# Moving the sums' loads to ScalarE, a wider use of the first slot group, fewer scatters between the last moves, and a bias added by DMA

## The chip, the core and the metric

The program runs on one core of one Trainium2 chip. The metric is the time of one execution in device microseconds (us), as the median of several runs. One execution was also recorded by the profiler; all rows below come from it.

## The reference, cut to what matters

The input `x` holds 8 sequences of 512 tokens with 256 numbers each (4096 tokens). Two layers follow each other, each with a layer norm ahead of it and a residual around it:

```python
x = x + attention(_layernorm(x), ...)        # only the first 16 rows of each sequence attend; every other row gets the bias "ob"
x = x + ffn(_layernorm(x), ...)              # per token: 4 of 32 experts and one shared expert
```

Inside `ffn` a router picks 4 experts for each token (`topk_idx`) and gives each a weight (`topk_w`). An expert is `down @ (silu(gate @ t) * (up @ t))` with an inner width of 128. The four results are multiplied by their weights, added, and the shared expert (width 256) is added on top. So there are 4096 * 4 = 16384 (token, expert) pairs.

For all rows but the first 16 of a sequence the attention gives zero, so that the first residual is `x + ob` with the bias row `ob`.

## The kernel before

The 4096 tokens are 32 tiles of 128. Tile 0 holds the 16 rows of each sequence that attend; tiles 1 to 31 hold the rest. `x_sb` keeps all of x in SBUF. x is loaded in five groups of tiles (`GROUPS_OF_TILES`, line 50): 1-4, 5-8, 9-16, 17-24 and 25-31; groups are counted from 0.

The work has two stages that overlap. In the **first stage** (0 to about 180 us) TensorE, ScalarE and VectorE do the attention of tile 0 as a chain of steps, and fill the time between the steps with other work in an order written out by hand (`FILL_PE`, `FILL_ACT`, `FILL_DVE`, lines 156 to 235). A letter with a number is an item: on VectorE `N0` to `N5` are the statistics of groups 3 and 4 (`statistic`, line 1543: bias, moments, root), `R` the pieces of the routing, `U` the products of the shared expert, `A` its additions. `N0` and `N3` add `ob` to the 8 and 7 tiles of groups 3 and 4 with one instruction each (`add_bias`, line 1277).

Every token row is then copied four times into DRAM, to a slot in the region of each of its experts. That is a **move**: ScalarE lays the normalised rows and their pair numbers into one of four groups of buffers in `xg` (`stage`, line 829), and GpSimd sends them out with four indirect DMAs per tile (`move(n)`, line 743, n = 0 to 31, tile 0 last). The 16 places of `xg` serve twice: moves use them as four groups of four, and the second stage loads its tiles into them.

In the **second stage**, the loop over expert tiles u (`part`), each u is 128 rows of one expert. 137 of them (`FIXED`) are certain. For each u, SyncE loads the rows from DRAM into a place of `xg` (`load_tile`, line 588), TensorE transposes them (`turn_x`, line 1175), multiplies by gate and up (`gate_up_of`) and by down (`down_of`), ScalarE copies and applies Silu (`keep_x`, `gate`, `keep_y`), VectorE copies the weights and makes the product (`hidden`), and GpSimd sends the result rows to `pairs_dram` with one indirect DMA, a **scatter** (`scatter(u)`, line 762). TensorE's order in the loop is gate and up of u, down of u - 1, turn of u + 2. The first 32 tiles need only the moves of token tiles 1 to 16; all later ones need every move. `place_of` (line 75) says which place a tile is loaded into: the first 24 go to places 0 to 7 (move groups 0 and 1), later ones around all 16. A place that held a tile before is free when that tile has been turned and its pair numbers kept (u below 63) or scattered (u from 63); a place that only moves have used is free when all the moves of its group have landed.

GpSimd's queue is one fixed order (lines 773 to 778): moves 0 to 28, then scatters between the last moves as `SOON` tells, then all other scatters.

The **sums**: VectorE adds the four weighted pair rows of a token tile to `x_sb` (`add_rows`, line 1805), in pairs of token tiles at the loop positions `SUM_AT`. The rows come back by loads of 512 KB into five buffers (`load_rows`, line 609). Ten pairs of such loads stand in SyncE's queue between its tile loads, at the positions `LOAD_AT` (79, 84, 90, ...); the first of them waits until every scatter below u = 63 has landed. SyncE also clears 128 rows behind each expert's region (`make_blank`, two per tile at u = 9 to 24), and stores finished groups.

```python
def place_of(u):
    return u % (RING // 2) if u < FIRST_LAPS else u % RING     # RING = 16, FIRST_LAPS = 24
```

Of the kernel before, what the change touches and what calls it, by code (L numbers as in the profile page):

```python
# [25 lines left out]
ALU = mybir.AluOpType  # L26
# [3 lines left out]
P = 128  # L30
# [4 lines left out]
TT = TOKENS // P  # L35
# [33 lines left out]
NARROW = 24  # L69


FIRST_LAPS = RING + RING // 2


def place_of(u):
# [24 lines left out]
KEPT = 63  # L100
# [18 lines left out]
def outs_used(k, n):  # L119
# [11 lines left out]
BEFORE_END = 24  # L131
SUM_ORDER = [*range(1, BEFORE_END + 1), 0, *range(BEFORE_END + 1, TT)]
EARLY_LOADS = 5
LOAD_AT = [79, 84, 90, 96, 110, 116, 121, 126, 131, 135]
assert STAGES[:2] == [PARTS[0][1] - 1, PARTS[1][1] - 1] and STAGES[3] == BEFORE_END and DONE_BY[3] < FIXED
assert all(at - RING + 1 >= DONE_BY[[2 * pair + 2 <= t for t in STAGES].index(True)] for pair, at in enumerate(LOAD_AT))
assert SUM_AT[-1] + TOPK <= FIXED and LOAD_AT[-1] < FIXED
SOON = {TT - 3: 4, TT - 2: 9, TT - 1: 14}
RANK_STEP = 2
STAGE_IN_LOOP = {0: 25, 2: 26, 5: 27, 8: 28, 11: 29, 15: 30, 18: 31}  # L140
ADD_IN_LOOP = {1: 12, 7: 13, 13: 14, 17: 15}
# [67 lines left out]
]  # L209
FILL_DVE = [  # L210
    "R0 R0 N6 R0 R0 R0 R0 P0 P1 P2 R0 R0 N0 U0 N1 N2 U1",
    "N3 N4 N5 R1 R1 R1",
    "R1 R1 R1 U2 U3",
    "R1",
    "U4 R1",
# [64 lines left out]
def build_program(nc, x, qkvo, gate_up, down, sh_gate_up, sh_down, router, rows, cols, local, out,  # L280
                  tokens_dram, pairs_dram):
    ctx = ExitStack()
    with ctx:
# [3 lines left out]
        def sem(name):  # L287
            return ctx.enter_context(nc.semaphore(name))
# [132 lines left out]

        att_x_in = sem("att_x_in")
        x_in = [sem(f"x_in{g}") for g in range(len(GROUPS_OF_TILES))]
        ob_in = sem("ob_in")
        router_in = sem("router_in")
        small_in = sem("small_in")
# [99 lines left out]
        def _(sp):  # L526
# [81 lines left out]

            def load_rows(q):

                if q == 0:
                    sp.wait_ge(pair_added, SHARED + 1)
                    for k in range(SHARED_OUTS[-1] + 1):
                        sp.wait_ge(scattered[k], 16 * outs_used(k, KEPT))
                elif q == 2:
                    sp.wait_ge(hid_ready, WEIGHTS_FROM + 2 * (3 * TOPK + 2) + 1)
                if q < BEFORE_END:
                    if q >= EARLY_LOADS:
                        sp.wait_ge(tile_summed, q - EARLY_LOADS + 1)
                    sp.dma_start(early4[q % EARLY_LOADS].rearrange("p k d -> p (k d)"), pair_tiles[:, SUM_ORDER[q], :]  # L620
                                 ).then_inc(early_in[q % EARLY_LOADS], 16)
                else:
                    sp.dma_start(load4[:, q - BEFORE_END].rearrange("p k d -> p (k d)"), pair_tiles[:, SUM_ORDER[q], :]
                                 ).then_inc(pairs_in[q - BEFORE_END], 16)
# [6 lines left out]
            for u in range(FIXED):  # L631
                if u == EARLY:
                    sp.wait_ge(moved_last, 16 * TOPK)
                    sp.wait_ge(tables_ready, 2)
                    sp.wait_ge(blanked, 16 * E)
                load_tile(u)
                for e in range(E):
                    if BLANKS_AT[e] == u:
                        make_blank(e)
                if u in LOAD_AT:  # L640
                    load_rows(2 * LOAD_AT.index(u))
                    load_rows(2 * LOAD_AT.index(u) + 1)
                if u == LOAD_AT[4]:
                    sp.wait_ge(tile_summed, 8)
                    store(*OUT_GROUPS[0])

# [30 lines left out]
        def _(pool):  # L677
# [60 lines left out]
            assert made[0] == N_CONSTS  # L738
            for what in ROOTS[3:]:
                inverse_root(what)  # L740


            def move(n):
# [50 lines left out]
        def _(act):  # L794
# [120 lines left out]
            def keep_y(u):  # L915
# [6 lines left out]
                    act.wait_ge(pair_added, 15)  # L922
                act.activation(yb[out_of(u)], y_ps(u), ACT.Copy).then_inc(y_ready, 1)  # L923

            def part(a, b):

                keep_x(a)
                keep_x(a + 1)
                for u in range(a, b):
                    if u in STAGE_IN_LOOP:  # L930
                        stage(STAGE_IN_LOOP[u])
                    gate(u)
                    if u > a:
                        keep_y(u - 1)
                    if u + 2 < b:
                        keep_x(u + 2)
                    if u == SHARE_STEP:
                        act.wait_ge(gate_done, SHARED + 1)
                        act.activation(pair_hid_0.rearrange("p m t -> p (m t)"), gate_0_ps, ACT.Silu
                                       ).then_inc(pair_silu_done, 1)  # L940
                keep_y(b - 1)
# [309 lines left out]
        def _(dve):  # L1251
# [291 lines left out]
            def statistic(k):  # L1543

                a, b = GROUPS_OF_TILES[3 + k // 3 % 2]
                if k in (0, 3):
                    add_bias(3 + k // 3)
                elif k in (1, 4):
                    moments(3 + k // 3)
                elif k == 6:  # L1550
                    shifts(*GROUPS_OF_TILES[2])
                else:
                    seq(dve.tensor_scalar(var_e[:, a:b], mv[:, a:b, 1:2].rearrange("p t a -> p (t a)"), EPS, None, ALU.add))
                    newton(rstd[:, a:b], var_e[:, a:b], half_root[:, 0:b - a])
                    dve.scalar_tensor_tensor(shift[:, a:b], mv[:, a:b, 0:1].rearrange("p t a -> p (t a)"), -1.0,
                                             rstd[:, a:b], ALU.mult, ALU.mult).then_inc(norm_ready, 1)
# [372 lines left out]
```

## Time and profile before

| | us |
|---|---|
| median of 3 runs | 443.57 |
| lowest and highest run | 441.66, 443.99 |
| the profiled execution | 442.9 |
| its span, first to last instruction | 441.1 |
| TensorE busy in the span | 363.4 (82%) |
| VectorE, ScalarE, GpSimd busy | 303.3, 238.5, 301.9 |

Engine names in the profile: PE is TensorE's matmul, PEld its weight load, DVE VectorE, ACT ScalarE, POOL GpSimd, SP SyncE; a q behind a name means its instruction queue. Times in rows are us from the start of the span unless marked ns. In a timeline a row is: start, length, engine, line, operation, out<-in, form, count, and in brackets the idle time before it with what ended it.

### The profile page before, as it was taken

The numbers are of one execution on the slowest core, as the hardware profiler recorded it, in microseconds if no ns is written. First come the engines' busy times: TensorE is split into PE (matmuls) and PEld (weight loads), VectorE is DVE, ScalarE is ACT, GpSimd is POOL, SyncE is SP. The second block draws the span as 40 slices with busy tenths as digits, with TensorE's granted clock in tenths as the row PEclk, the third lists the DMA queues.
The fourth block names the chain that finished last, engine by engine and source line by source line (L and its number), as shares of the span: only waits on it lengthen the run. The fifth ranks groups of instructions, "written<-read, shape, count | busy, mean of one in ns | idle before, by whom it ended". The sixth has DMA issues, their size and how long they took to land.

```text
span 441.1 us, 9457 instructions
## 1 busy us (share of the span) xinstructions
PE 363.4 (82%) x2368; PEld 295.4 (67%) x2368; DVE 303.3 (69%) x1097; ACT 238.5 (54%) x612; POOL 301.9 (68%) x438
## 2 busy tenths in 40 slices
PE   0468899999788898799959999999999999999200
PEld 0354666757346455588849899999989989998200
DVE  3669995963997965367524468885477847887847
ACT  1454693578564656557725566556555656655100
POOL 5511888677887887877878777777777776666300
PEclk9999996999999999999989999999999999999855
DMA  7990233432228968778965885652798898997796
GB/s 168 250 332 24 90 115 115 155 119 92 111 103 330 397 243 273 266 234 274 291 200 170 274 241 152 186 173 97 255 308 282 293 328 278 340 292 250 264 309 214
DMA packets 47033, 98.01 MB, mean 222 GB/s; under 512 B 8697, under 2 KB 30846, under 8 KB 45696
## 3 DMA queue, kind: packets, MB, share of 16 engines
q1 hardware_dynamic: 33968, 62.70, 45.9%
q0 software_dynamic: 12720, 34.62, 21.1%
q8 instruction: 23, 0.38, 0.4%
q14 instruction: 34, 0.28, 0.2%
q10 hardware_dynamic: 288, 0.03, 0.1%
HBM read 53.93 MB, written 44.57 MB: 223 GB/s over the span
## 4 chain that ended last, share of the span: by engine, by line
PE 63%; DVE 15%; DMA 9%; issue 4%; ACT 3%; POOL 3%; SPq 1%; POOLq 0%; DVEq 0%; ACTq 0%
PE two_banks L1192 24%; PE two_banks L1205 12%; PE two_banks L1016 7%; PE two_banks L1179 6%; PE two_banks L1067 5%; DMA loopb<-slots_dram 3%; PE two_banks L971 3%; DVE x_sb L1816 3%; DMA slots_dram<-loopb,slot_i 2%; PE two_banks L965 2%; DMA gu_w<-pairs_dram 1%; DMA pairs_dram<-routing,loopb 1%; POOL pairs_dram L766 1%; PE two_banks L1151 1%; DVE loopb L1599 1%
## 5 line engine op out<-in xcount | busy, mean ns | idle before, releaser
L756 POOL DMA_INDIRECT slots_dram<-loopb,slot_i x128 | 129.0, 1008 | 49.3 <-issue 25.4
L1192 PE MATMUL two_banks<-routing,staged_w 128*128 128x128 f32 x1096 | 145.8, 276 | 0.1
L1192 PEld LDWEIGHTS two_banks<-routing,staged_w 128*128 128x128 f32 x1096 | 134.1, 193 | 0.4 <-ACT routing L908 0.4
L1205 PE MATMUL two_banks<-dn_w,routing 128*128 x274 | 83.3, 386 | 1.5 <-DVE routing L1802 1.3
L1802 DVE TENSOR_TENSOR routing<-routing,two_banks 128x128 f32<-128x128 f32 x137 | 39.1, 286 | 65.6 <-ACT routing L913 59.2
L1842 DVE COPY staged_w<-gu_w 128x512 f32 x137 | 62.2, 455 | 15.7 <-issue 12.4
L913 ACT ACTIVATE routing<-two_banks 128x128 f32<-128x128 f32 x137 | 38.0, 277 | 57.6 <-PE two_banks L1192 57.5
L1016 PE MATMUL two_banks<-gu_w,sgu_w 128*128 128x512 f32 (+1 forms) x128 | 63.1, 624 | 3.1 <-DVE loopb L1599 2.3
L1179 PE MATMUL two_banks<-ident,loopb 128*128 128x128 f32 x274 | 52.9, 275 | 10.3 <-DMA loopb<-slots_dram 8.9
L908 ACT ACTIVATE routing<-two_banks 128x256 f32<-128x256 f32 x137 | 52.0, 380 | 13.3 <-PE two_banks L1179 13.3
L766 POOL DMA_INDIRECT pairs_dram<-routing,loopb x44 | 45.7, 1038 | 17.4 <-issue 15.3
L1179 PEld LDWEIGHTS two_banks<-ident,loopb 128*128 128x128 f32 x274 | 38.0, 142 | 26.0 <-DMA loopb<-slots_dram 10.7
L1205 PEld LDWEIGHTS two_banks<-dn_w,routing 128*128 128x128 f32 x274 | 41.8, 193 | 3.4 <-issue 3.0
L766 POOL DMA_INDIRECT pairs_dram<-routing,stats x33 | 35.0, 1059 | 9.7 <-issue 7.3
L841 ACT ACTIVATE loopb<-x_sb,shift,rstd 128x1024 f32<-128x1024 f32 x32 | 39.5, 1234 | 2.8 <-DMA slots_dram<-loopb,slot_i 2.7
L1016 PEld LDWEIGHTS two_banks<-gu_w,sgu_w 128*128 128x128 f32 x128 | 24.0, 203 | 25.2 <-issue 18.4
L923 ACT ACTIVATE routing<-two_banks 128x256 f32<-128x256 f32 x77 | 29.6, 384 | 13.9 <-PE two_banks L1205 13.9
L965 PE MATMUL two_banks<-ident,gu_w 128*128 128x128 f32 x62 | 14.8, 337 | 22.2 <-POOL gu_w L736 15.9
L1067 PE MATMUL two_banks<-sdn_w,loopb 128*128 128x256 f32 x124 | 30.2, 386 | 3.2 <-ACT gu_w L880 1.3
L965 PEld LDWEIGHTS two_banks<-ident,gu_w 128*128 128x128 f32 x62 | 9.8, 183 | 28.5 <-POOL gu_w L736 15.8
L1067 PEld LDWEIGHTS two_banks<-sdn_w,loopb 128*128 128x128 f32 x124 | 22.6, 190 | 8.5 <-issue 3.5
L766 POOL DMA_INDIRECT pairs_dram<-sgu_w,loopb x20 | 20.0, 999 | 8.2 <-issue 7.5
(302 smaller groups left out, 514.6 us busy)
## 6 DMA issues: line engine op xcount, KB each, us to landing
loopb<-slots_dram SPq DMA_DIRECT2D x137, 128.5 KB, 2.8
routing<-pairs_dram SPq DMA_DIRECT2D x14, 512.0 KB, 5.3
loopb<-pairs_dram SPq DMA_DIRECT2D x10, 512.0 KB, 4.4
slots_dram<-blank SPq DMA_DIRECT2D x33, 136.0 KB, 27.1
gu_w<-in_gate_up SPq DMA_DIRECT2D x2, 2048.0 KB, 10.7
gu_w<-pairs_dram SPq DMA_DIRECT2D x8, 512.0 KB, 7.8
gu_w<-in_gate_up SPq DMA_DIRECT2D x6, 512.0 KB
x_sb<-in_x SPq DMA_DIRECT2D x2, 1024.0 KB, 13.9
```

The source lines that it names most:

```text
L756: pool.indirect_dma_start(out=slots_dram, out_offset=bass.IndirectOffsetOnAxis(ap=slot_i[:, at:at + 1], axis=0), in_=xg[:, r, :] if n < TT ...
L766: pool.indirect_dma_start(out=pairs_dram, out_offset=bass.IndirectOffsetOnAxis(ap=(kept_ids[:, u:u + 1] if u < KEPT else xg[:, place_of(u) ...
L841: act.activation(rows_of[:, :, 0:D], x_sb[:, t, :].unsqueeze(1).to_broadcast([P, TOPK, D]), ACT.Identity, bias=shift[:, t:t + 1], scale=rs ...
L908: act.activation(xT[:, u % 2], turn_ps[u % 2], ACT.Copy).then_inc(xT_ready, 1)
L913: act.activation(silu[:, u % 2, 0:I], bank[2 + u % 2][:, 0:I], ACT.Silu).then_inc(silu_done, 1)
L1016: ins = pe.matmul(o[:, 0:n], weights[:, m, c, :], xnT[:, 4 * q:4 * q + n // P, c, :], start=(c == 0), stop=(c == KC - 1))
L1067: ins = pe.matmul(pair_y_ps[:, i, :], pair_hid[:, m, t:t + P], sdn_w[:, m, :], start=(m == 0), stop=(m == 1))
L1179: ins = pe.transpose(turn_ps[u % 2][:, c, :], xg[:, place_of(u), c * P:(c + 1) * P], ident[:, :])
L1192: ins = pe.matmul(bank[2 + u % 2][:, m * P:(m + 1) * P], staged_w[:, u % 2, c, m * I:(m + 1) * I], xT[:, u % 2, c, :], start=(c == 0), sto ...
L1205: ins = pe.matmul(y_ps(u), hid[:, u % 2, 0:P], w, start=True, stop=True)
L1802: dve.tensor_tensor(hid[:, u % 2, 0:I], silu[:, u % 2, 0:I], bank[2 + u % 2][:, I:2 * I], ALU.mult).then_inc(hid_ready, 1)
L1842: dve.tensor_copy(staged_w[:, u % 2].rearrange("p c i -> p (c i)"), gu_w[:, bass.ds(ids[first][u % EIDS], 1)].rearrange("p a c i -> p (a c ...
```

## The change

There are four parts. Ten pairs of sums' loads leave SyncE's queue for ScalarE's, where they stand ahead of `gate(u)` at slightly smaller positions, with their waits; the store of tiles 1 to 8 stays in SyncE's queue at u = 116. Tiles 24 to 31 are loaded into places 0 to 7. Eight scatters instead of fourteen stand between the last moves. The two bias additions of groups 3 and 4 leave VectorE; GpSimd issues two DMAs that add the bias row to `x_sb` in flight, after its own constants and roots and ahead of move 0, and VectorE waits for them ahead of the moments.

```diff
-FIRST_LAPS = RING + RING // 2
+FIRST_LAPS = 2 * RING
...
-LOAD_AT = [79, 84, 90, 96, 110, 116, 121, 126, 131, 135]
+LOAD_AT = [76, 81, 86, 91, 104, 109, 114, 119, 124, 129]
+STORE_AT = 116
...
-SOON = {TT - 3: 4, TT - 2: 9, TT - 1: 14}
+SOON = {TT - 3: 2, TT - 2: 5, TT - 1: 8}
...
-    "R0 R0 N6 R0 R0 R0 R0 P0 P1 P2 R0 R0 N0 U0 N1 N2 U1",
-    "N3 N4 N5 R1 R1 R1",
+    "R0 R0 N6 R0 R0 R0 R0 P0 P1 P2 R0 R0 U0 N1 N2 U1",
+    "N4 N5 R1 R1 R1",
...
+        bias_added = [sem(f"bias_added{g}") for g in (3, 4)]
...
             def load_rows(q):
 
-                if q == 0:
-                    sp.wait_ge(pair_added, SHARED + 1)
-                    for k in range(SHARED_OUTS[-1] + 1):
-                        sp.wait_ge(scattered[k], 16 * outs_used(k, KEPT))
-                elif q == 2:
-                    sp.wait_ge(hid_ready, WEIGHTS_FROM + 2 * (3 * TOPK + 2) + 1)
...
-                if u in LOAD_AT:
-                    load_rows(2 * LOAD_AT.index(u))
-                    load_rows(2 * LOAD_AT.index(u) + 1)
-                if u == LOAD_AT[4]:
+                if u == STORE_AT:
                     sp.wait_ge(tile_summed, 8)
                     store(*OUT_GROUPS[0])
...
+            for g, (a, b) in list(enumerate(GROUPS_OF_TILES))[3:]:
+                pool.wait_ge(ob_in, 16)
+                pool.wait_ge(x_in[g], 16)
+                pool.dma_start(x_sb[:, a:b, :], row("ob").unsqueeze(1).to_broadcast([P, b - a, D]), accum_op=ALU.add
+                               ).then_inc(bias_added[g - 3], 16)
...
+            def load_early(q):
+
+                if q == 0:
+                    act.wait_ge(pair_added, SHARED + 1)
+                    for k in range(SHARED_OUTS[-1] + 1):
+                        act.wait_ge(scattered[k], 16 * outs_used(k, KEPT))
+                elif q == 2:
+                    act.wait_ge(hid_ready, WEIGHTS_FROM + 2 * (3 * TOPK + 2) + 1)
+                for stage_of, t in enumerate(STAGES[:2]):
+                    if q == t:
+                        for k in OUTS:
+                            act.wait_ge(scattered[k], 16 * outs_used(k, DONE_BY[stage_of + 1]))
+                if q >= EARLY_LOADS:
+                    act.wait_ge(tile_summed, q - EARLY_LOADS + 1)
+                act.dma_start(early4[q % EARLY_LOADS].rearrange("p k d -> p (k d)"), pair_tiles[:, SUM_ORDER[q], :]
+                              ).then_inc(early_in[q % EARLY_LOADS], 16)
+
             def part(a, b):
...
                 for u in range(a, b):
+                    if u in LOAD_AT:
+                        load_early(2 * LOAD_AT.index(u))
+                        load_early(2 * LOAD_AT.index(u) + 1)
...
                     gate(u)
...
-                if k in (0, 3):
-                    add_bias(3 + k // 3)
-                elif k in (1, 4):
+                if k in (1, 4):
+                    dve.wait_ge(bias_added[k // 3], 16)
                     moments(3 + k // 3)
```

## Rows read from the trace of the kernel before

**Rows 1.** Busy time by stretch: length, busy us (count) by engine, PE clock, DMA share, GB/s.

```profile
260.00:280.00 20.00, 20.00 (x157) 18.69 (x157) 16.87 (x54) 12.10 (x40) 15.73 (x15) 1.00 0.58 172
...
228.60:231.60 3.00, 3.00 (x12) 2.75 (x13) 0.26 (x2) 0.66 (x2) 2.39 (x3) 0.50 0.85 243
```

**Rows 2.** Timeline of PE: around tiles 24, 32, 79 and 85, and at 51 us.

```profile
222.52 0.60 PE L1205 MATMUL two_banks<-dn_w,routing 128*128 x2
228.60 0.69 PE L1179 MATMUL two_banks<-ident,loopb 128*128 128x128 f32 x2 [5.49 <-DMA loopb<-slots_dram]
...
243.76 0.44 PE L1179 MATMUL two_banks<-ident,loopb 128*128 128x128 f32 x2 [1.09 <-DMA loopb<-slots_dram]
...
316.47 0.38 PE L1179 MATMUL two_banks<-ident,loopb 128*128 128x128 f32 x2
...
326.80 0.44 PE L1179 MATMUL two_banks<-ident,loopb 128*128 128x128 f32 x2 [0.86 <-DMA loopb<-slots_dram]
...
51.37 1.99 PE L1067 MATMUL two_banks<-sdn_w,loopb 128*128 128x256 f32 x8 [0.32 <-DVE loopb L1599]
```

**Rows 3.** The chain of waits, its transfers: start, length, what.

```profile
238.69 2.43 DMA slots_dram<-loopb,slot_i
...
241.60 2.12 DMA loopb<-slots_dram
...
321.29 5.47 DMA loopb<-slots_dram
```

**Rows 4.** Timeline of POOL around its last moves: scatters (L766) and moves (L756).

```profile
206.59 1.03 POOL L766 DMA_INDIRECT pairs_dram<-routing,stats  x1 [0.19 <-issue]
...
211.80 0.97 POOL L756 DMA_INDIRECT slots_dram<-loopb,slot_i  x1 [0.30 <-ACT loopb L923]
...
216.87 1.00 POOL L766 DMA_INDIRECT pairs_dram<-routing,stats  x1 [0.19 <-issue]
```

**Rows 5.** Timeline of SP's queue: blanks, tile loads (L599) and sums' loads (L620).

```profile
219.77 0.85 SPq L576 DMA_DIRECT2D slots_dram<-blank  x2
226.28 0.35 SPq L599 DMA_DIRECT2D loopb<-slots_dram  x1
...
309.91 0.33 SPq L599 DMA_DIRECT2D loopb<-slots_dram  x1
310.98 0.83 SPq L620 DMA_DIRECT2D loopb<-pairs_dram  x2
```

**Rows 6.** Timeline of POOL: scatter 63, the first with ids from its place.

```profile
307.26 0.98 POOL L766 DMA_INDIRECT pairs_dram<-routing,loopb  x1 [0.30 <-issue]
```

**Rows 7.** Scatters (line L766) between 284 and 309.5 us, issue to landing.

```profile
DMA to landing us min/median/max: 2.5/2.5/2.5
```

**Rows 8.** The same line between 311 and 345 us.

```profile
DMA to landing us min/median/max: 4.1/5.1/6.2
```

**Rows 9.** Timeline of DVE: the two bias additions.

```profile
41.55 2.28 DVE L1281 TENSOR_TENSOR x_sb<-x_sb,row_sb 128x2048 f32<-128x2048 f32 x1
...
51.83 2.01 DVE L1281 TENSOR_TENSOR x_sb<-x_sb,row_sb 128x1792 f32<-128x1792 f32 x1
```

**Rows 10.** Timeline of POOL: its last root, the first two indirect DMAs of the moves.

```profile
25.58 1.64 POOL L697 TENSOR_TENSOR rstd<-var_e,half 128x8 f32<-128x8 f32 x1 [6.11 <-DVE var_e L1269]
41.95 2.99 POOL L756 DMA_INDIRECT slots_dram<-loopb,slot_i  x1 [14.73 <-DVE slot_i L1392]
...
45.24 0.96 POOL L756 DMA_INDIRECT slots_dram<-loopb,slot_i  x1 [0.17 <-issue]
```

**Rows 11.** The five loads of x (line L530): issue ns, first and last start; landing.

```profile
L530 SPq DMA_DIRECT2D x_sb<-in_x x5: 542/597/663, 2.1 to 7.1; - x5
...
DMA to landing us min/median/max: 6.4/11.7/22.7
```

**Rows 12.** Timeline of ACT in the steady loop: Silu of one tile.

```profile
300.78 0.28 ACT L913 ACTIVATE routing<-two_banks 128x128 f32<-128x128 f32 x1 [0.45 <-PE two_banks L1192]
```

**Rows 13.** Sums' loads (line L620) in SP's queue: count, issue ns min/median/max.

```profile
L620 SPq DMA_DIRECT2D routing<-pairs_dram x14: 319/424/1311, 319.2 to 411.1; - x14
```

More of the change, by code:

```diff
@@ L133 @@
 EARLY_LOADS = 5
-LOAD_AT = [79, 84, 90, 96, 110, 116, 121, 126, 131, 135]
+LOAD_AT = [76, 81, 86, 91, 104, 109, 114, 119, 124, 129]
+STORE_AT = 116
 assert STAGES[:2] == [PARTS[0][1] - 1, PARTS[1][1] - 1] and STAGES[3] == BEFORE_END and DONE_BY[3] < FIXED
-assert all(at - RING + 1 >= DONE_BY[[2 * pair + 2 <= t for t in STAGES].index(True)] for pair, at in enumerate(LOAD_AT))
+assert all(at > DONE_BY[[2 * pair + 2 <= t for t in STAGES].index(True)] for pair, at in enumerate(LOAD_AT))
 assert SUM_AT[-1] + TOPK <= FIXED and LOAD_AT[-1] < FIXED
-SOON = {TT - 3: 4, TT - 2: 9, TT - 1: 14}
+SOON = {TT - 3: 2, TT - 2: 5, TT - 1: 8}
 RANK_STEP = 2
```

## The prediction

> **What bounds the kernel now.** I read the busy time by stretch first. In the steady loop TensorE is busy for all of 20 us, every other engine for less, and the clock is at its full 2.4 GHz (granted 1.00) [rows 1]. So a tile costs what TensorE needs for it: from the turn of tile 32 (243.76) to that of tile 85 (326.80) the timeline of PE gives 243.76 to 316.47 for 47 tiles, 1.546 us each [rows 2]. What can be won is where PE stands still. The timeline and the chain of waits show three such places around the change:
>
> - Tile 24: PE waits 5.49 us for the tile's load, then runs some 3 us at the lower clock level, 1.2 GHz (granted 0.50) [rows 1, 2].
> - Tile 32: 1.09 us, again for a load. Its load went out at 241.60, behind the landing of the last move (238.69 + 2.43) [rows 2, 3].
> - Tile 85: 0.86 us; its load took 5.47 us, issued behind two sums' loads [rows 2, 3].
>
> In the first stage PE waits 0.32 us for VectorE at 51 us [rows 2]; VectorE's two bias additions stand ahead of that, 2.28 and 2.01 us [rows 9].
>
> **Tiles 24 to 31 in places 0 to 7, and eight scatters between the moves.** These belong together, since the second sets when tile 32 can start and the first when tile 24 can.
>
> Tile 24 no longer waits for moves of the third group to land, which let its load go at 226.28 [rows 5], but for the turn of tile 16, long past. Its load then stands behind the last blanks on SP's queue, done at 219.77 + 0.85 = 220.6 [rows 5]. With 0.4 to issue and 2.1 to land (a load without neighbours, [rows 3]) it is there near 223.3; PE wants it at 228.60 - 5.49 = 223.1 [rows 2]. Eight tiles later, 8 x 1.546, PE is at 235.7. The lower clock goes with the wait.
>
> Tile 32 needs every move. Six scatters fewer stand ahead of the last move. Four scatters and the idle between them take (216.87 - 211.80) = 5.07 for a move's four DMAs, and (211.80 - 206.59) = 5.21, 1.30 each, for scatters [rows 4]; six are 7.8 us. Load 32 goes out at 241.60 - 7.8 = 233.8 and lands 2.1 later, 235.9. Both limits agree on about 236.0, so tile 32 turns 243.76 - 236.0 = 7.7 us earlier.
>
> **Where that lead ends.** The six scatters are not gone: they are issued after the last move, and POOL's queue has the same moves and scatters ahead of scatter 63 as before. POOL is the engine that runs without a pause here, so scatter 63 stays at 307.26 [rows 6]. From tile 79 on, a place is free only when its former tile (u - 16) was scattered, because the scatter reads its ids there: load 79 went out at 309.91, 2.65 after scatter 63 began [rows 5, 6]. Tile 79 can be turned 2.3 after that at the earliest, 312.2, against 316.47 now [rows 2]. So at least 7.7 - 4.3 = 3.4 us of the lead are lost, and PE stands still for them.
>
> What is left depends on how long scatters take to land. Between 284 and 309.5 us they land in 2.5 us [rows 7]; from 311 on, with sums' loads under way, in a median of 5.1 [rows 8]. In the changed kernel the first pair of sums' loads waits for the same scatters as now (below 63, landed by about 308.5) and goes out on ScalarE near 309.6, just when the scatters 64 and on are in flight. Scatter 64 begins at 307.26 + 1.30 = 308.56; with 5.1 it lands at 313.7, tile 80 is loaded 0.2 + 2.5 later, 316.4, against 316.47 + 1.55 = 318.0 now: lead 1.6. Scatter 65: 309.9 + 5.1 + 2.7 = 317.7 against 319.6, lead 1.9. I take **1.5 us**; bounds are 4.3 (landing stays at 2.5) and 0 (6.2 as in the top of [rows 8], with a slow load behind). After that a tile (1.546) costs more than a scatter (1.30), so the slack grows and the lead is kept to the end.
>
> A rule of the Trainium skill bears on this, *DMA: Bandwidth & Descriptors*, section "Issuing engines are not separate DMA queues": transfers issued by several engines share the same 16 DMA engines, and another issuer saves only sequencer time. [Rows 8] agree as far as scatters of POOL are slowed by loads of SP. By it the next item would be worth nothing, and the sum 1.3 instead of 2.3; that lies between the forecast and B.
>
> **Sums' loads on ScalarE.** SP's tile load no longer queues behind two 512-KB loads of its own queue, which made load 85 land in 5.47 instead of 2.12 [rows 3]. The stall of tile 85, about **+1.0** with its wait of 0.86, goes; bounds 0 (the transfers share the engines whatever the queue) and 1.0. ScalarE pays: two issues at 0.42 each (0.83 for the pair in [rows 5]; median 0.424, longest 1.311 in [rows 13]) ahead of a Silu that has 0.45 us of idle before it [rows 12]. ScalarE works 16.87 of 20 us [rows 1], so a pair delays one gate by about 0.4 and the next tiles catch up. Over ten pairs I take **-0.5**; bounds 0 and -3 (every pair at the long issue and nothing caught up). What queues behind a wait here is worse than on SP: a pair that waits for scatters or for a free buffer holds `gate`, `keep_y`, `keep_x`, and so PE. For the first pair that wait lies inside the stall already counted at tile 79.
>
> **Bias by accumulating transfers.** 4.3 us leave VectorE [rows 9], but PE waited for it only 0.32 [rows 2]: **+0.3**, bounds 0 and 4.3. POOL is free for the two new DMAs from 25.58 + 1.64 = 27.2 and idle for 14.73 before its first move DMA [rows 10]; the second needs x's last group, landed by 7.1 + 22.7 = 29.8 [rows 11]. No row shows POOL issuing a plain accumulating transfer. Nearest is an indirect one of 128 rows of 1 KB, 0.96 [rows 10]; 8 and 7 tiles are 8 and 7 such, 7.7 and 6.7 us. From below, 0.96 each. At the upper end POOL is done at 29.8 or 34.9 + 6.7 = 41.6, just ahead of its first move (41.95). I take no loss.
>
> **Sum.** 1.5 + 1.0 + 0.3 - 0.5 = 2.3 us. The profiled execution took 442.9 (span 441.1); 442.9 - 2.3 = 440.6. The median of the runs stands 0.7 above it, which gives 441.3; between them I say **441.0**.
>
> **Rivals.**
>
> *A, landings stay short.* If loads on another queue don't slow scatters, the lead at tile 79 is the full 4.3: 4.3 + 1.0 + 0.3 = 5.6, about 437.5. For it: [rows 7] has tile loads running beside scatters at 2.5. Against it: [rows 8], where the only newcomer is the sums' loads.
>
> *B, the lead is eaten.* Scatters landing at 6.2 and loads behind them at 5.5 leave tile 80 at 308.6 + 6.2 + 0.2 + 5.5 = 320.5, later than today's 318.0. Then nothing of the 7.7 is left and PE waits at 79 to 85 instead of 24; the stall of 85 is exchanged for these: about 443.3, no change. For it: load 85 itself took 5.47 [rows 3].
>
> *C, slower: the bias lands late.* VectorE used to end the first addition at 41.55 + 2.28 = 43.8 [rows 9]; without it, it reaches the moments some 2.3 us sooner, but now waits there for the transfer. The next product of the shared expert is queued behind that wait, and PE waits for it at 51.37 [rows 2]. The break-even is a landing near 44.5; each us later costs one. POOL issues the first DMA at 27.2, or later, if POOL makes it more slowly than 0.96 per tile: [rows 10] show the first move's DMA at 2.99 instead of 0.96 while VectorE adds the bias beside it [rows 9], three times as long. At three times 7.7 us the first transfer lands at 27.2 + 23 = 50, 5.5 late: 2.3 - 5.5 = -3.2, about 446. Against it: VectorE's long additions are those that go. [...]
>
> *D, the edits do not do what they say.* Tile 24 might still wait, if its load stands behind blanks that are themselves late; the lead at 32 would be 1 to 2 us, under the 4.3 that tile 79 passes on, so the end is that of B or of the forecast. It needs no time of its own.
>
> **How the numbers follow.** Forecast 0.48, A 0.17, B 0.18, C 0.12, 0.05 for anything else. The forecast's own range, from lead 0.5 to 3 and ScalarE's cost 0 to -1.5, is 439 to 443. To leave out 2 in 10 the range must take in most of A and B and the near side of C: **436 to 446**. A measurement of this kernel tells 0.5%, 2.2 us, from no change, so the border to faster is 441.4, close to the forecast. Faster: half of the forecast's chance and a little (0.27), A (0.17), some of the rest: 0.45. Slower, above 445.8: most of C, a fifth of B, and the far bound of ScalarE's issues: 0.17. The same: 0.38.
>
> **What would show it.** Right: tile 24 turned near 223.5 and tile 32 near 236 without half clock; scatter 63 at 307 to 308; a new stall of PE at tiles 79 to 82, for a load behind a scatter; sums' loads on ACTq from about 309.6 and scatters landing in over 4 us beside them; no wait at 85; VectorE waiting under 1 us for the bias. Wrong: scatters landing in 2.5 beside the row loads (A); PE's turn of tile 85 no earlier than 326 (B); VectorE idle ahead of the moments of group 3 and PE's product of 51.37 later than that (C); PE waiting for ScalarE at each pair of sums' loads, which would put my -0.5 wrong.

## The result and the profile after

| | before | after |
|---|---|---|
| median, first set (4 runs each) | 442.7 us | 447.09 us (443.99 to 448.74) |
| ratio, first set | | 1.0098, 95% interval 1.0055 to 1.0142 |
| median, second set (32 and 12 runs) | 441.75 us | 443.78 us (437.76 to 449.18) |
| ratio, second set | | 1.0064, interval 1.0027 to 1.0101 |
| the profiled execution | 442.9 us, span 441.1 | 443.99 us, span 442.3 |

The change makes the kernel slower: both intervals lie above 1. The price is small and not well known, 4.4 us by the medians of the first set and 2.0 us (0.46%) by those of the second. Some executions are over 1.5% longer than the shortest of their kernel; without them the second set's medians, 442.5 and 441.6 us, are too close to be told apart. Two versions below that keep the change's loads and stores in the loop are slower too (bias_dve 1.0045, store_late 1.0064). The profiled execution of the changed kernel is the shortest of its first four, so its trace shows where time goes, not the whole of it.

The page of the changed kernel: busy time, the tenths of 40 slices (11 us each) for TensorE, and its granted clock.

```profile
span 442.3 us, 9473 instructions
PE 367.0 (83%) x2368; PEld 298.5 (67%) x2368; DVE 301.1 (68%) x1095; ACT 237.6 (54%) x612; POOL 303.6 (69%) x440
...
PE   0468899999888997898999999999699997998400
...
PEclk9998999999989999899999999999699998999955
```

The hole at 229 us of the kernel before [rows 1] is gone. There are new ones near 315 us (PE 6, clock 6) and near 370 us (PE 7). Line 1197 is the turn that was line 1179. The timeline of PE, at tiles 0, 24, 32, then 79, 80, 81, 85, then the product of tile 109, the turns of tiles 112 and 113, and the product of tile 129:

```profile
178.27 0.79 PE L1197 MATMUL two_banks<-ident,loopb 128*128 128x128 f32 x4 [1.83 <-DMA loopb<-slots_dram]
...
223.18 0.38 PE L1197 MATMUL two_banks<-ident,loopb 128*128 128x128 f32 x2
...
235.96 0.33 PE L1197 MATMUL two_banks<-ident,loopb 128*128 128x128 f32 x1 [0.26 <-DVE routing L1819]
...
313.39 0.69 PE L1197 MATMUL two_banks<-ident,loopb 128*128 128x128 f32 x2 [3.85 <-DMA loopb<-slots_dram]
...
316.43 0.63 PE L1197 MATMUL two_banks<-ident,loopb 128*128 128x128 f32 x2
...
319.21 0.38 PE L1197 MATMUL two_banks<-ident,loopb 128*128 128x128 f32 x2
...
325.40 0.38 PE L1197 MATMUL two_banks<-ident,loopb 128*128 128x128 f32 x2
...
367.69 0.69 PE L1223 MATMUL two_banks<-dn_w,routing 128*128 x2 [0.77 <-DVE routing L1819]
370.11 0.59 PE L1197 MATMUL two_banks<-ident,loopb 128*128 128x128 f32 x2 [1.73 <-issue]
...
373.05 0.63 PE L1197 MATMUL two_banks<-ident,loopb 128*128 128x128 f32 x2
...
403.99 0.69 PE L1223 MATMUL two_banks<-dn_w,routing 128*128 x2 [1.17 <-DVE routing L1819]
```

Against [rows 2] tile 24 comes 5.4 us earlier and tile 32 7.8 us. Tile 79 comes only 3.1 us earlier, tile 81 (before: 316.47 + 2 x 1.546 = 319.56) 0.35, tile 85 1.4. Tile 113 is then some 2 us later than before. In the kernel before, the second pair of sums' loads stood in SyncE's queue just ahead of load 85:

```profile
319.25 1.79 SPq L620 DMA_DIRECT2D routing<-pairs_dram  x2
```

The clock in the first hole, and the busy time in the second (length, busy us and count by engine, clock, DMA share, GB/s):

```profile
313.00:319.20 6.20, 5.81 (x24) 5.38 (x25) 0.84 (x3) 1.71 (x5) 4.71 (x5) 0.52 0.75 225
...
364.00:372.00 8.00, 5.50 (x36) 4.77 (x35) 4.24 (x12) 2.56 (x9) 4.61 (x5) 0.89 1.00 273
```

What stands around the second hole: SP's queue issues the store of tiles 1 to 8, 1 MB, at 362.89 (the loads above it are those of tiles 79 and 80). The change had moved this store too, from behind load 110 to behind load 116.

```profile
308.78 0.33 SPq L601 DMA_DIRECT2D loopb<-slots_dram  x1
...
313.63 0.33 SPq L601 DMA_DIRECT2D loopb<-slots_dram  x1
...
362.89 0.62 SPq L608 DMA_DIRECT2D out<-x_sb  x1
```

ScalarE issues its sixth pair of sums' loads 1.6 us later, its tenth near 400:

```profile
364.52 0.33 ACTq L937 DMA_DIRECT2D loopb<-pairs_dram  x1
...
364.89 1.96 ACTq L937 DMA_DIRECT2D loopb<-pairs_dram  x1
366.95 0.28 ACT L911 ACTIVATE routing<-two_banks 128x128 f32<-128x128 f32 x1 [1.99 <-PE two_banks L1210]
...
400.79 2.36 ACTq L937 DMA_DIRECT2D routing<-pairs_dram  x1
...
403.25 0.28 ACT L911 ACTIVATE routing<-two_banks 128x128 f32<-128x128 f32 x1 [2.40 <-PE two_banks L1210]
```

The second issue of each of these pairs took 1.96 and 2.36 us where one takes 0.39 in the median. Silu of that tile waited behind it: the row puts the 1.99 down to PE, which had been done for 1.6 us. The "issue" that PE waits for at 370.11 has a name too. Every four tiles PE and VectorE read expert numbers from an SBUF table into registers. The source view of that line for the changed kernel (count, ns minimum, median, maximum), for VectorE's read (line 1850) in the window 366 to 369, and the same line of the kernel before:

```profile
L1233 PEldq TENSOR_LOAD <-tables x35: 327/333/2233, 175.4 to 410.0; - x35
...
L1850 DVEq TENSOR_LOAD <-tables x1: 2043/2043/2043, 368.0 to 368.0; - x1
```

```profile
L1215 PEldq TENSOR_LOAD <-tables x35: 328/387/1778, 177.2 to 406.6; - x35
...
L1215 PEldq TENSOR_LOAD <-tables x1: 1778/1778/1778, 355.2 to 355.2; - x1
```

A read of 0.33 us took 2.23, behind the store. In the kernel before it took 1.78, at 355.2, again behind a store:

```profile
353.65 0.62 SPq L606 DMA_DIRECT2D out<-x_sb  x1
```

TensorE waited 0.80 us for it at tile 104, and 0.53 us at tile 132 for a read of 1.54 us behind the second store (1.65 us of time together). The prediction names neither.

```profile
357.19 0.41 PE L1179 MATMUL two_banks<-ident,loopb 128*128 128x128 f32 x2 [0.80 <-issue]
...
401.21 0.41 PE L1179 MATMUL two_banks<-ident,loopb 128*128 128x128 f32 x2 [0.53 <-issue]
```

POOL in the changed kernel: the two accumulating transfers, the first move's DMA, and scatter 63.

```profile
27.07 1.82 POOL L737 DMA_DIRECT2D x_sb<-row_sb  x1
29.90 1.74 POOL L737 DMA_DIRECT2D x_sb<-row_sb  x1 [1.01 <-ACT loopb L841]
41.84 1.14 POOL L754 DMA_INDIRECT slots_dram<-loopb,slot_i  x1 [10.20 <-DVE slot_i L1410]
...
305.94 1.19 POOL L764 DMA_INDIRECT pairs_dram<-routing,loopb  x1 [0.30 <-issue]
```

Landing of scatters (line 764) between 311 and 345 us, against 4.1/5.1/6.2 in [rows 8]:

```profile
DMA to landing us min/median/max: 3.1/3.7/4.4
```

The end, in the chain of waits: the last scatter and the last sums' load, of the changed kernel and of the one before.

```profile
416.41 4.82 DMA pairs_dram<-routing,loopb
...
421.93 4.71 DMA gu_w<-pairs_dram
```

```profile
412.94 5.38 DMA pairs_dram<-routing,loopb
...
419.02 6.43 DMA gu_w<-pairs_dram
```

The last scatter is 3.5 us later than before; shorter transfers give 2.3 of it back, so that the span is 1.2 longer.

### The profile page after: what moved, and what is told of

It reads as the page before. It is cut to its first block, busy times and chain, and to the rows that moved or that the text cites. A ratio compares the mean times of both kernels' runs of the same rounds, so it can differ in the third digit from the quotient of the medians.

```text
span 442.3 us, 9473 instructions
## 1 busy us (share of the span) xinstructions
PE 367.0 (83%) x2368; PEld 298.5 (67%) x2368; DVE 301.1 (68%) x1095; ACT 237.6 (54%) x612; POOL 303.6 (69%) x440
## 3 DMA queue, kind: packets, MB, share of 16 engines
q1 hardware_dynamic: 31088, 52.22, 39.1%
## 4 chain that ended last, share of the span: by engine, by line
PE 61%; DVE 10%; POOL 10%; DMA 8%; issue 6%; ACT 2%; ACTq 1%; SPq 0%; DVEq 0%; POOLq 0%
PE two_banks L1210 25%; PE two_banks L1223 12%; PE two_banks L1197 6%; PE two_banks L1034 6%; POOL slots_dram L754 6%; PE two_banks L989 4%; DMA slots_dram<-loopb,slot_i 3%; DVE x_sb L1833 3%; PE two_banks L1085 2%; DMA loopb<-slots_dram 2%; PE two_banks L983 2%; DMA pairs_dram<-routing,loopb 2%; POOL pairs_dram L764 1%; DMA gu_w<-pairs_dram 1%; DVE gu_w L1383 1%
## 5 line engine op out<-in xcount | busy, mean ns | idle before, releaser
L754 POOL DMA_INDIRECT slots_dram<-loopb,slot_i x128 | 126.7, 990 | 47.3 <-issue 28.1
L1210 PE MATMUL two_banks<-routing,staged_w 128*128 128x128 f32 x1096 | 149.0, 280 | 0.1
L1210 PEld LDWEIGHTS two_banks<-routing,staged_w 128*128 128x128 f32 x1096 | 137.4, 197 | 0.5 <-ACT routing L906 0.4
L1223 PE MATMUL two_banks<-dn_w,routing 128*128 x274 | 84.3, 390 | 4.2 <-DVE routing L1819 4.2
L1819 DVE TENSOR_TENSOR routing<-routing,two_banks 128x128 f32<-128x128 f32 x137 | 39.1, 285 | 71.4 <-ACT routing L911 65.3
L1859 DVE COPY staged_w<-gu_w 128x512 f32 x137 | 64.2, 469 | 12.9 <-issue 8.9
L1197 PE MATMUL two_banks<-ident,loopb 128*128 128x128 f32 x274 | 53.8, 279 | 7.9 <-DMA loopb<-slots_dram 5.7
L906 ACT ACTIVATE routing<-two_banks 128x256 f32<-128x256 f32 x137 | 52.0, 380 | 11.3 <-PE two_banks L1197 10.8
L764 POOL DMA_INDIRECT pairs_dram<-sgu_w,loopb x20 | 21.2, 1059 | 9.3 <-issue 6.2
## 6 DMA issues: line engine op xcount, KB each, us to landing
gu_w<-in_gate_up SPq DMA_DIRECT2D x2, 2048.0 KB, 10.7
```

Source lines behind the costliest of these rows:

```text
L754: pool.indirect_dma_start(out=slots_dram, out_offset=bass.IndirectOffsetOnAxis(ap=slot_i[:, at:at + 1], axis=0), in_=xg[:, r, :] if n < TT ...
L764: pool.indirect_dma_start(out=pairs_dram, out_offset=bass.IndirectOffsetOnAxis(ap=(kept_ids[:, u:u + 1] if u < KEPT else xg[:, place_of(u) ...
L906: act.activation(xT[:, u % 2], turn_ps[u % 2], ACT.Copy).then_inc(xT_ready, 1)
L1197: ins = pe.transpose(turn_ps[u % 2][:, c, :], xg[:, place_of(u), c * P:(c + 1) * P], ident[:, :])
L1210: ins = pe.matmul(bank[2 + u % 2][:, m * P:(m + 1) * P], staged_w[:, u % 2, c, m * I:(m + 1) * I], xT[:, u % 2, c, :], start=(c == 0), sto ...
L1223: ins = pe.matmul(y_ps(u), hid[:, u % 2, 0:P], w, start=True, stop=True)
```

## The experiments

Theory P: the stall at tile 79 and the lower clock behind it (granted 0.52) eat the lead. Theory S: the 1-MB store makes ScalarE's issues and register loads last 2 us. Rivals: L (sums' loads hold ScalarE wherever stores are) and B (the accumulating transfers cost it). All ratios are to the kernel before (23 to 35 runs of it, 9 to 12 of each version).

| label | edit | median us | ratio, 95% interval |
|---|---|---|---|
| again | the changed kernel | 443.78 | 1.0064, 1.0027 to 1.0101 |
| loads_sp | change without ScalarE's loads | 441.91 | 0.9987, 0.9953 to 1.0021 |
| bias_dve | change without the bias transfers | 444.67 | 1.0045, 1.0012 to 1.0077 |
| store_late | change, first store after the loop's tile loads | 444.22 | 1.0064, 1.0034 to 1.0093 |
| stores_tail | change, both stores behind the last sums' loads | 445.17 | 1.0056, 1.0022 to 1.0089 |
| only_loads | before + ScalarE's loads | 443.42 | 1.0017, 0.9985 to 1.0050 |
| only_places_soon | before + places and fewer scatters | 442.86 | 1.0009, 0.9966 to 1.0051 |
| only_bias | before + bias transfers | 441.80 | 0.9989, 0.9951 to 1.0026 |
| ids_all | change, ids of all tiles kept | 443.72 | 1.0041, 1.0006 to 1.0077 |
| ids_stores_tail | ids_all + stores_tail | 439.42 | 0.9941, 0.9909 to 0.9973 |
| ids_stores_end | ids_all, stores behind loads 20 to 23 | 439.63 | 0.9966, 0.9931 to 1.0001 |
| ids_small_stores | ids_all, stores of 256 KB | 436.97 | 0.9908, 0.9870 to 0.9946 |
| small_stores | change, stores of 256 KB | 440.48 | 0.9967, 0.9924 to 1.0010 |
| small_stores_before | before, stores of 256 KB | 442.53 | 0.9994, 0.9951 to 1.0037 |

**again** (no edit).

> The changed kernel once more, for a second trace and more times. Theory S (the 1-MB output store of tiles 1 to 8 now meets a sums' load on ScalarE, and both a DMA issue on ScalarE and a register load on TensorE last 2 us in its time): 445 to 448 us, and in the second trace again a loss of 3 to 5 us at tiles 109 to 115, with a register load or an issue of 1.5 us or more behind the store. Theory L (the sums' loads hold ScalarE wherever they stand): the same time, but losses spread over the ten pairs. Theory N (noise between executions): within 0.5% of before.

The ratio is 1.0064. Its interval leaves out "no change" but not theory N's 0.5%, and the median, 443.78, lies under the range of S and L. In this trace, of the shortest of the 12 executions (437.76 us), the clash at tiles 114 to 116 costs 1.1 us (a register load of 1.48 us on VectorE, one of 1.22 on TensorE, an issue of 0.92), not the 3 to 5 that S expected; the one at tile 132 costs 1.8 (an issue of 2.11), 1.6 in the first trace. How hard a store hits differs between executions.

**loads_sp, bias_dve**: one part of the change undone in each.

```diff
-                    if u in LOAD_AT:
-                        load_early(2 * LOAD_AT.index(u))
-                        load_early(2 * LOAD_AT.index(u) + 1)
```
```diff
-                if k in (1, 4):
-                    dve.wait_ge(bias_added[k // 3], 16)
+                if k in (0, 3):
+                    add_bias(3 + k // 3)
+                elif k in (1, 4):
```

> The changed kernel with the sums' loads and the store where they were, on SyncE. Theories S and L: 440 to 443 us, since nothing of ScalarE's queue waits and the store is again behind load 110; tile 79 still stalls near 312. Theory B (the accumulating transfers cost the time): 446 to 448, as with the whole change.

> The changed kernel with the two bias additions back on VectorE. Theories S and L: 446 to 449, as with the whole change or 1 us slower, since the first tile's turn comes 1.5 us later. Theory B: 442 to 443.

With the loads back on SyncE the slowdown is gone (0.9987); with the bias back on VectorE it stays (1.0045, a median between the two ranges). Theory B falls: the loss needs the loads' move. The move includes their positions and that of the store, which loads_sp puts back too; no run has the loads on SyncE and the store at load 116.

**store_late, stores_tail**: the stores moved.

```diff
-                if u == STORE_AT:
-                    sp.wait_ge(tile_summed, 8)
-                    store(*OUT_GROUPS[0])
...
+            store(*OUT_GROUPS[0])
+            store(*OUT_GROUPS[1])
             for a, b in OUT_GROUPS[3:]:
```

> The changed kernel with the store of tiles 1 to 8 issued after the loop's tile loads, just ahead of that of tiles 9 to 16, instead of behind load 116. Theory S: the stall at tiles 112 to 114 is gone, tile 120 is turned some 2 us earlier than before the change and the time is 441 to 444 (the store's megabyte now lies near the end). Theory L: 446 to 448, the lead goes at the pairs as before.

> The changed kernel with both stores of the loop (tiles 1 to 8 and 9 to 16) moved behind the last sums' loads. Theory S (a 1-MB store makes the DMA issues and register loads that fall into its time last about 2 us, and ScalarE's issues are now among them): no issue or register load above 1 us between 320 and 410 us, the losses at tiles 112 to 117 and 128 to 134 gone, and 440 to 442 us. Theory L (sums' loads hold ScalarE wherever stores are): 444 to 446, with the losses still at the pairs.

Both times missed what theory S expected, and that of stores_tail lies in L's range; the traces speak for S. In store_late the stall at 112 to 114 is gone, but the first store now goes out at 390.7, 5.2 us ahead of the second, and tiles 128 to 134 lose 4.9 us. In stores_tail the register loads of TensorE from 320 us on, and ScalarE's issues, are:

```profile
L1230 PEldq TENSOR_LOAD <-tables x14: 327/334/634, 326.1 to 406.8; - x14
...
L934 ACTq DMA_DIRECT2D routing<-pairs_dram x12: 326/386/532, 324.4 to 399.2; - x12
L934 ACTq DMA_DIRECT2D loopb<-pairs_dram x8: 327/398/484, 311.2 to 391.5; - x8
```

None is above 0.64 us, and TensorE loses nothing after tile 81: from the turn of tile 85 to that of tile 136 it takes 79.1 us, against 85.4 in the changed kernel and 80.6 in the one before. But the end pays it back (timeline of SP):

```profile
424.62 1.84 SPq L608 DMA_DIRECT2D out<-x_sb  x3
...
431.69 6.87 SPq L608 DMA_DIRECT2D out<-x_sb  x3
```

The first row is both moved stores and one more, the second the last three stores, issued up to 438.6; the span ends at 445.1. The kernel before issues the same last three at the same time and ends at 441.1. So without stores the loop is 6.3 us shorter than in the changed kernel's trace, and a store at the end delays the last ones.

**only_loads, only_places_soon, only_bias**: one part of the change each, in the kernel before. The edits are the change's own lines; of the second:

```diff
-FIRST_LAPS = RING + RING // 2
+FIRST_LAPS = 2 * RING
-SOON = {TT - 3: 4, TT - 2: 9, TT - 1: 14}
+SOON = {TT - 3: 2, TT - 2: 5, TT - 1: 8}
```

> The kernel before with the sums' loads on ScalarE and the store at 116 alone. Theories S and L: 444 to 446, 2 to 3 us slower than before. Theory P (what costs is the stall at tile 79 with the half clock behind it, and it comes from the earlier tiles and fewer scatters, not from the loads): 441 to 443.

> The kernel before with tiles 24 to 31 in places 0 to 7 and eight scatters between the moves, alone. Theory P (the lead of nearly 8 us ends at tile 79, where a new stall and the half clock behind it give most of it back): tile 32 turned some 8 us earlier than in the kernel before, tile 85 within 3 us of it, and 441 to 444. If the lead lasted: 436 to 439.

> The kernel before with the bias added by the two accumulating transfers, alone. Theory: 1 us sooner at the first tile's turn and no more, 441 to 443. Theory B (the transfers cost what the change lost): 444 to 446.

Alone, no part can be told from no change; only_loads lies under what S and L expected and just above P's range. only_bias does not turn the first tile 1 us sooner, as expected, but at 180.33, 0.6 later than before. The parts add up to +0.15% with an interval of about 0.65 on either side, so whether the whole is more than its parts stays open. only_places_soon shows theory P in its trace, turns of tiles 79, 80 and 81:

```profile
309.64 0.44 PE L1179 MATMUL two_banks<-ident,loopb 128*128 128x128 f32 x2 [1.90 <-DMA loopb<-slots_dram]
...
315.18 0.44 PE L1179 MATMUL two_banks<-ident,loopb 128*128 128x128 f32 x2 [3.77 <-DMA loopb<-slots_dram]
317.41 0.63 PE L1179 MATMUL two_banks<-ident,loopb 128*128 128x128 f32 x2
```

A lead of 9.0 us at tile 32 is 2.2 at tile 81.

**ids_all, ids_stores_tail**: VectorE keeps the ids of all 137 tiles, so that a place is free when its tile was turned.

```diff
+IDS = FIXED
-                    if v < KEPT:
+                    if v < IDS:
                         sp.wait_ge(ids_kept, v + 1)
```

> The changed kernel, in which VectorE keeps a copy of the row ids for all 137 tiles instead of the first 63, so that a place is free once its tile was turned and copied, not scattered. Theory P: no stall at tile 79, tile 79 is turned some 7 us earlier than in the kernel before and most of that lead lasts to tile 104: 436 to 440 us. Its rival (the lead is lost anyway, at the output buffers that scatters must free or at the sums): 443 to 445.

> Both of the last edits in one: ids of all tiles kept, and no store in the loop. Theories P and S together: 433 to 438 us, turn of tile 136 at 398 to 402. If only one of them holds, 438 to 441.

ids_all alone gains little (1.0041, and 443.72 us lies in the rival's range): the lead of 6.9 us lasts to tile 104, as theory P has it, and is lost there. The waits of PE and of ACT in its loop:

```profile
PE two_banks L1224 <- DVE routing L1820: 8.4, 4, 4.2
```
```profile
ACT routing L912 <- DMA pairs_dram<-sgu_w,stats: 6.1, 1, 6.1
```

The fifth pair on ScalarE waits 6.1 us for the scatters it reads, and `gate` waits behind it. The last of these scatters begins at 349.5, just behind a store issued at 348.7, and the pair goes out 8.3 us later; in ids_stores_tail, with no store there, it goes out 3.1 us after that scatter. Without stores in the loop the two edits together give 0.9941, 1.2% less than stores_tail: theory P's price, seen once nothing else takes the lead. But 439.42 us lies in the range set for one theory alone, not in that for both. The turn of tile 79 there has no stall and comes 8.5 us ahead of [rows 2]:

```profile
307.95 0.38 PE L1195 MATMUL two_banks<-ident,loopb 128*128 128x128 f32 x2
```

Tile 136 is turned at 397.3 (407.4 before), sooner than expected; the tail, 39.1 us from there against 33.7, takes 5.4 of it.

**ids_stores_end, ids_small_stores**: with all ids kept, the stores behind the loads of sums 20 to 23, or cut.

```diff
             for q in range(IN_LOOP, BEFORE_END):
                 load_rows(q)
+            sp.wait_ge(tile_summed, 8)
+            store(*OUT_GROUPS[0])
+            sp.wait_ge(tile_summed, 16)
+            store(*OUT_GROUPS[1])
```

```diff
-OUT_GROUPS = [(1, 9), (9, 17), (17, 21), ...
+OUT_GROUPS = [*[(a, a + 2) for a in range(1, 17, 2)], (17, 21), ...
+STORE_AT = [101, 106, 111, 116, 128, 133]
...
+                if u in STORE_AT:
+                    pair = STORE_AT.index(u)
+                    sp.wait_ge(tile_summed, 2 * pair + 2)
+                    store(*OUT_GROUPS[pair])
```

> All ids kept, and the two stores between the loop's last tile loads and the last scatter's landing (behind the loads of sums 20 to 23) instead of in the loop. Theory S, T (a store in the tail is paid again, because it delays the last loads and the last stores): the loop as short as with the stores in the tail, the tail 3 to 5 us shorter than there, 434 to 438. Rival: the last scatters land later by as much, 439 to 441.

> All ids kept, and the two stores of 1 MB each cut into eight of 256 KB, one behind each pair of sums, six in the loop and two after it. Theory S in its narrow form (only a megabyte at once makes issues and register loads take 2 us): none above 1 us, the loop within 2 us of that without stores, and 433 to 438. Rival (every store does it, whatever its size): several short clashes, 440 to 443.

At the loop's end the stores delay the last scatter's landing (408.8 to 418.4, 9.7 us instead of 5.4): the rival's price, and 0.9966. Cut into 256 KB they make the best version of the study, 436.97 us, 0.9908. The time is in the range of S, but both signs of its narrow form fail: one issue of ScalarE still took 2.11 us, at 383.7, 2.8 behind a small store, and from tile 85 to 136 the loop takes 82.6 us, 2.7 more than without stores.

**small_stores, small_stores_before**: the same cut in the changed kernel and in the kernel before, with places as they were.

```diff
-STORE_AT = 116
+STORE_AT = [101, 106, 111, 116, 128, 133]
```

> The changed kernel as it is, with its two 1-MB stores cut into eight of 256 KB (places of ids as in the change, so the stall at tile 79 stays). Theory S as the whole cause: the 0.7 per cent are gone, 440 to 443 us. Theory P as the cause with S small: 443 to 446, as with the change; the stall at 79 to 81 takes 6 to 8 us as before.

> The kernel before with its two 1-MB stores cut into eight of 256 KB. Theory S: the two pauses of TensorE for a register load at tiles 104 and 132 (1.65 us together) are gone, 440 to 441.5. Rival (eight stores clash as often as two): 442 to 444.

In the changed kernel the cut brings 1.0064 to 0.9967, with intervals that do not meet; in the kernel before it brings nothing (442.53, the rival's range; register loads of 1.05 and 1.69 us still stand 1.1 and 1.7 us behind a small store). By the times, the slowdown comes from the change and the big stores together. The trace of small_stores does not show this gain. It is of one of the longest executions (445.72 us) and has no issue on ScalarE above 0.8 us; yet tiles 109 to 114 lose 4.7 us in it, as much as in the changed kernel (4.6), begun by a second price of ScalarE's queue (timeline of DVE and PE, at the product of tile 109 and the turn of tile 112):

```profile
367.75 0.49 DVE L1835 SCALAR_TENSOR_TENSOR x_sb<-routing,wts,x_sb 128x256 f32<-128x256 f32 x1 [2.83 <-DMA routing<-pairs_dram]
...
368.58 0.69 PE L1225 MATMUL two_banks<-dn_w,routing 128*128 x2 [2.21 <-DVE routing L1821]
...
370.01 0.66 PE L1199 MATMUL two_banks<-ident,loopb 128*128 128x128 f32 x2 [0.74 <-issue]
```

The rows of the fifth pair were issued at 357.1 and landed 10.7 us later, after VectorE wanted them; its product for TensorE was queued behind that wait. SyncE had issued this pair at 352.5 in the kernel before. The 0.74 is a register load again, of 1.15 us, 3.1 behind a small store.

The 16 traces together say more than any one time. From the turn of tile 85 to that of tile 136 the undisturbed loop takes 51 x 1.547 = 78.9 us; what each trace takes above that:

| sums' loads on | stores in the loop | lost, us | traces |
|---|---|---|---|
| SyncE | 1 MB | 1.1 to 2.5 | before, loads_sp, only_places_soon, only_bias |
| SyncE | 256 KB | 1.2 | small_stores_before |
| ScalarE | 1 MB | 3.2 to 11.3 | changed kernel (twice), bias_dve, store_late, only_loads, ids_all |
| ScalarE | 256 KB | 3.7 and 5.1 | ids_small_stores, small_stores |
| ScalarE | none | 0.2 to 1.0 | stores_tail, ids_stores_tail, ids_stores_end |

So in these traces a loss above 2.5 us needs both, sums' loads on ScalarE and stores beside them, and theory L falls. (7.9 of the 11.3 us of ids_all lie at its wait for scatters.) Cut stores still cost in the loop; why the time is better with them, no trace shows.

## Why the prediction was wrong

- **Tiles 24 and 32: right.** Forecast 223.3 and 236.0, measured 223.18 and 235.96.
- **Where the lead ends: right in place and cause, wrong in price.** Tile 79 waits 3.85 us for a load behind a scatter, as said. Scatter 63 did not stay at 307.26 but began at 305.94 (304 to 310 in the other traces), and the load went out 1.1 us sooner than before, at 308.78. It took 4.6 us to be used beside the row loads instead of the 2.3 I gave it, so the lead at tile 79 is 3.1 (ceiling 4.3). What I left out is the clock. I had noted 3 us at 1.2 GHz behind the stall at tile 24 [rows 1], and let them go with that stall without charging the new one: tiles 79 to 81 took 5.82 us instead of 3.09, 2.7 lost at a granted 0.52. The forecast lead of 1.5 was 0.35.
- **Scatters at 6.2 beside row loads, loads behind them: not so.** They landed in a median of 3.7 in 311 to 345 us, against 5.1 before. Loads of ScalarE's queue slowed scatters less, not more. Rival B's end, no lead left, all but came true at tile 81, yet by the clock and not by landings.
- **Tile 85: right.** +1.0, the stall is gone: tiles 81 to 85 lose 0.7 to 1.8 us in all five traces with these loads on SyncE and at most 0.2 in all eleven with them on ScalarE. The Trainium skill, *DMA: Bandwidth & Descriptors*, section "Issuing engines are not separate DMA queues", has another issuer save only the sequencer's time. The issues of the second pair held SyncE's queue for 1.79 us ahead of load 85, so the trace does not contradict this; worth nothing, as the prediction read it, it was not at this place. For the part as a whole (only_loads, 1.0017) that reading is not far off.
- **ScalarE pays 0.5: the step that failed.** I took the issue at its median and let the next tiles catch up; even the bound, -3, took 1.3 as the longest issue. From tile 85 to 136 the change lost 4.8 us (85.4 against 80.6). Eight of the ten pairs cost 0.8 us each, but two of them 2.3 and 2.7, and what stands behind a late gate is the PE's product, VectorE's, and PE's next register load. Tiles 112 to 114 lost 2.9 + 1.4 + 0.3 = 4.6 us, the second figure at a granted clock of 0.52; tiles 121 to 132 lost 1.9, where the kernel before lost 0.7. The kernel before already had two pauses of this kind (tiles 104 and 132, "issue" in its waits); the prediction passed over them and so never asked what a store does to short instructions. The change put a third short instruction, ScalarE's issue, into the same stretch. The table of the 16 traces supports this, and so does the time of small_stores, but not its trace; the time of stores_tail shows that moving stores away is not free.
- **Bias: rival C was wrong.** The transfers held POOL for 1.82 and 1.74 us, not 7, and landed at 40.6 and 45.2, ahead of VectorE's moments at 42.3 and 50.4. The first move's DMA fell from 2.99 to 1.14; it is 2.99 in all five traces with the addition on VectorE beside it and 1.14 in all eleven without. The Trainium skill, *SBUF — State Buffer*, section "Who interferes with whom", has a VectorE instruction with two SBUF inputs contend with a GpSimd instruction that reads SBUF, and not with one that only writes it. The addition has two such inputs and the move's DMA reads its slots from SBUF, so the rows agree. Of the two additions only the first stood ahead of the product at 51.37; the second began at 51.83. The first turn came 1.5 us sooner in this trace, but 0.6 later in only_bias, so no run shows a gain.
- **The sum.** By the trace: 7.8 at tile 32, -7.4 at 79 to 81, +1.0 at 85, +1.0 at 104 (whose pause lay elsewhere), -4.6 at 112, -1.2 at 128 to 132, +2.2 in the tail, together -1.2, against +2.3 forecast. These are differences of two single executions; the tail takes 31.4 to 33.9 us in the ten traces with 1-MB stores in the loop, so its +2.2 need not come from the change. The side of the forecast and the range (436 to 446) were both missed in the first set's median; the second set's 443.78 lies in the range, with a ratio above 1.

## What to carry to other kernels

A lead won by removing a stall is worth only what the next resource lets through, and a new stall on TensorE is to be charged with the clock behind it, 2.7 us at tiles 79 to 81 here. An "issue" in a profile is an instruction with a name: find it before calling it unchanged, and ask what falls into the same stretch when another engine begins to issue there. DMA issues moved to an engine on the critical path cost here up to their longest time, not their median, where a store ran beside them; cutting the stores gave better times than moving them.

## What the hardware showed that I had not expected

Small instructions that do not use a large transfer's data become slow beside it. A register read from SBUF of 0.33 us took 1.5 to 2.2 at its longest in each of the ten traces with 1-MB stores in the loop, and under 1 us from tile 79 to 136 in the three without stores there. A DMA issue of ScalarE, 0.39 in the median, took 1.9 to 3.1, mostly within 6 us of such a store's issue. Loads of 512 KB alone, in the three traces without stores in the loop, did not show it; stores of 256 KB did, with reads of up to 1.7 us and one issue of 2.1. Of 13 issues of ScalarE above 0.9 us in these traces, three had no store in the 6 us ahead. Why the store does it, no run shows. And one program's executions differ by more than I assumed: the kernel before ran from 437.67 to 448.99 us, which is why single traces here are read for places and prices, and only the ratios for the time.
